# Cross attention of a fused decoder: power per projection, context rounding and output projection later, input quantisation over two groups

## What is computed

```python
def _div_clamp_fp8(x, scale):
    y = jnp.clip(x / scale, -448.0, 448.0)
    y = y.astype(jnp.bfloat16).astype(jnp.float32)
    return y.astype(jnp.float8_e4m3fn).astype(jnp.float32)
def _fp8_linear_pertensor(x, wq, w_scale, in_scale):
    xq = _div_clamp_fp8(x, in_scale)
    return jnp.einsum('bsi,oi->bso', xq * in_scale, wq) * w_scale
...
ln_out = _ln(hidden_states, ln_w, ln_b)
q = _ln(_fp8_linear_pertensor(ln_out, wq, ...).reshape(b, s, g, hpg, d), qln_w, qln_b)
k = _ln(_fp8_linear_pertensor(ln_out, wk, ...).reshape(b, s, g, d), kln_w, kln_b)
v = _fp8_linear_pertensor(ln_out, wv, ...).reshape(b, s, g, d)
core = _gqa(q, k, v).reshape(b, s, nh * d)
qx = _ln(_fp8_linear_pertensor(ln_out, wqx, ...).reshape(b, s, g, hpg, d), qxln_w, qxln_b)
kx, vx = jnp.split(jnp.einsum('bsi,oi->bso', cond, w_kv_x), 2, axis=-1)
kx = _ln(kx.reshape(b, sc, g, d), kxln_w, kxln_b)
xout = _gqa(qx, kx, vx.reshape(b, sc, g, d)).reshape(b, s, nh * d)
catq = _div_clamp_fp8(jnp.concatenate([core, xout], axis=-1), proj_smooth)
return jnp.einsum('bsi,oi->bso', catq, wproj) * (proj_in_scale * proj_w_scale)
```

## Time and profile before

| | us |
|---|---|
| median of 3 runs | 1294.21 |
| lowest, highest | 1289.71, 1295.01 |
| the profiled execution | 1295.41 |
| its span in the profile | 1293.6 |
| PE / DVE / ACT / POOL busy | 1026.7 / 902.1 / 607.4 / 448.1 |
| mean granted TensorE clock | 0.907 of full |

### The profile page before, as it was taken

The page is one execution under the profiler, slowest core; times in us unless marked ns, Lnnn a source line. Parts: engine busy times, 40 slices in busy tenths (PEclk is TensorE's granted clock), DMA queues, the critical chain, the costliest instruction groups (busy, mean ns, idle before and its releaser), DMA issues.

```text
span 1293.6 us, 15285 instructions
## 1 busy us (share of the span) xinstructions
PE 1026.7 (79%) x5194; PEld 639.5 (49%) x5204; DVE 902.1 (70%) x1501; ACT 607.4 (47%) x1457; POOL 448.1 (35%) x247
## 2 busy tenths in 40 slices
PE   5998876365556766477878899899887799999998
PEld 3777732124122222245556566666655465555555
DVE  4567689887699998887887877676888444333222
ACT  2444461065566651365566667777566223111111
POOL 0012244050076640256666645445554422000000
PEclk9879789777778787699999999999998899999999
DMA  9500000401000000000000062000003000000000
GB/s 339 220 1 1 1 0 0 133 15 26 0 1 1 0 0 1 1 1 1 1 1 2 1 159 66 2 1 2 1 1 115 1 1 1 1 17 1 1 1 17
DMA packets 23773, 36.56 MB, mean 28 GB/s; under 512 B 3584, under 2 KB 19904, under 8 KB 22592
## 3 DMA queue, kind: packets, MB, share of 16 engines
q1 hardware_dynamic: 23696, 35.58, 8.4%
HBM read 34.53 MB, written 1.05 MB: 28 GB/s over the span
## 4 chain that ended last, share of the span: by engine, by line
PE 37%; DVE 22%; ACT 10%; issue 8%; POOL 1%; DVEq 0%; ACTq 0%; POOLq 0%
PE ps L2150 12%; PE ps L2174 8%; DVE arena L979 6%; PE ps L1725 3%; DVE arena L975 3%; PE ps L1709 3%; ACT arena L1024 3%; PE ps L1699 2%; PE ps L1692 2%; ACT arena L2004 2%; DVE arena L1831 2%; PE ps L1738 2%; DVE arena L1825 2%; PE ps L2162 1%; PE ps L1717 1%
## 5 line engine op out<-in xcount | busy, mean ns | idle before, releaser
L2198 DVE TENSOR_TENSOR arena<-arena,ps 128x512 f32<-128x512 f32 (+1 forms) x56 | 38.5, 687 | 151.3 <-ACT arena L2238 151.3
L2238 ACT ACTIVATE arena<-ps,arena 128x512 f32<-128x512 f32 (+1 forms) x56 | 38.4, 687 | 167.5 <-PE ps L2150 167.5
L1058 PE MATMUL ps<-arena,ident 128*128 128x512 f32 x128 | 83.9, 791 | 37.6 <-DVE arena L984 37.6
L1995 ACT ACTIVATE arena<-ps,arena 128x512 f32<-128x512 f32 x96 | 68.1, 775 | 88.3 <-PE ps L1699 88.0
L2174 PE MATMUL ps<-wide,arena 128*128 128x256 f32 (+1 forms) x448 | 106.2, 380 | 0.0
L2066 POOL TENSOR_TENSOR arena<-arena 128x1024 f32<-128x1024 bf16 x32 | 67.9, 2122 | 107.8 <-DVE arena L1638 107.8
L2077 POOL TENSOR_TENSOR arena<-arena 128x12 f32<-128x12 f32 x32 | 73.1, 2283 | 91.9 <-DVE arena L1836 91.7
L2004 ACT ACTIVATE arena<-ps,arena 128x128 f32<-128x128 f32 x256 | 91.1, 383 | 22.8 <-DVE arena L1816 22.8
L2150 PE MATMUL ps<-XT,wide 128*128 128x512 f16 (+1 forms) x384 | 93.3, 380 | 0.6 <-DVE X L1866 0.6
L2174 PEld LDWEIGHTS ps<-wide,arena 128*128 128x128 f32 (+1 forms) x448 | 84.9, 190 | 17.7 <-issue 1.6
L1717 PE MATMUL ps<-ident,arena 128*128 128x128 f32 x256 | 44.0, 297 | 56.1 <-DVE arena L1825 55.7
(11 more groups left out here) (319 smaller groups left out, 2439.2 us busy)
## 6 DMA issues: line engine op xcount, KB each, us to landing
side<-in_wproj SPq DMA_DIRECT2D x1, 4096.0 KB, 14.2
wide<-in_w_down SPq DMA_DIRECT2D x1, 3584.0 KB, 12.7
wide<-in_w_gate SPq DMA_DIRECT2D x2, 1728.0 KB, 12.1
side<-in_w_up SPq DMA_DIRECT2D x3, 1024.0 KB, 9.3
arena<-in_taps SPq DMA_DIRECT2D x1, 2048.0 KB, 15.7
wide<-in_wq SPq DMA_DIRECT2D x1, 2048.0 KB, 10.6
wide<-in_wqx SPq DMA_DIRECT2D x1, 2048.0 KB, 16.0
wide<-in_w_kv_x SPq DMA_DIRECT2D x1, 2048.0 KB, 24.0
```

The source lines that it names most:

```text
L1058: last = pe.matmul(ps[:, 4 + 2 * c + j, :], k.ident[:, :], read[i % 2][:, 512 * j:512 * j + 512], start=(n == 0), stop=(n == NST - 1), ski ...
```

## The change

Power: `root` is called per projection, with 4 columns each; the keys' epsilon is added on POOL, those of the queries stand as a 129th column in the squares' tile, so that the reduction adds them, and `sum_eps` goes. DVE does `variance(g+1, 1)` between the two `biggest`, and `variance(g+1, 2)` behind both `divide`. ACT does `square(g+1, 2)` behind `weigh(g, 1)`. POOL does the three `root` first and then `add_c(g-1)`, `round_c(g-1)`; `cm` has two buffers. `project_out(g, 0)` moves from turn g+1 to turn g+2. `scale_x` moves to even groups, behind `clip`, `quantise_x` and `add_x` stay in odd groups (`quantise_x` behind `clip`, `add_x` a group earlier than before), `round_x` stays in even groups, now behind `round_c`. `turn_x` and `take_x` move a turn. `add_out` and the experts' variance move behind `normalise`.

```diff
FP8_ROUND = 1.5 * 2.0 ** 20
 FP8_LEAST = 2.0 ** -6
 NEG = -1e30
-MOE_AT = 15296
+MOE_AT = 15824
 def wait(eng, sem, n):
...
     xq = [A.take([3, KC * S], BF16) for _ in range(2)]
     xqx = k.XT[:, 1, :].bitcast(BF16).rearrange("p (b n) -> p b n", b=B)
     qn = A.take([3, BLK])
-    sq = A.take([2, BLK])
+    sq = A.take([2 * MAXB, HD + 1])
     sq_k = A.take([MAXB, HD], BF16)
...
     cy = A.take([QH, S], BF16)
-    cm = A.take([QH, S], BF16)
+    cm = [A.take([QH, S], BF16) for _ in range(2)]
     cs = A.take([QH, S])
     cq = [A.take([QH, S], BF16) for _ in range(2)]
     norms = A.take([8])
...
     xq_ready = k.sem("xa_xq_ready")
     proj_psum = k.sem("xa_proj_psum")
     sq_ready = k.sem("xa_sq_ready")
-    var_ready = k.sem("xa_var_ready")
     rs_ready = k.sem("xa_rs_ready")
     qn_ready = k.sem("xa_qn_ready")
     turn_psum = k.sem("xa_turn_psum")
...
         for j in range(3):
             turn(0, j)
         turn_x(1)
+        turn_x(2)
         for g in range(NG):
             nxt = g + 1 < NG
             if nxt:
...
                 moe.turn_comb(pe, 0, ps[:, 6, :])
             turn_p(g, 0)
             if g >= 2:
-                project_out(g - 2, 1)
+                project_out(g - 2, 0)
             turn_p(g, 1)
             mix(g, 0)
+            if g >= 2:
+                project_out(g - 2, 1)
             mix(g, 1)
-            if g >= 1:
-                project_out(g - 1, 0)
             if nxt:
                 for j in range(3):
                     turn(g + 1, j)
-            if g % 2 == 0 and g // 2 + 2 < B:
-                turn_x(g // 2 + 2)
+            if g % 2 and (g + 5) // 2 < B:
+                turn_x((g + 5) // 2)
             if g == 25:
                 moe.total_tensor(pe, ps[:, 6, :])
             if g in (26, 27):
                 moe.logits(pe, 0, g - 26, ps[:, 6, :])
+        project_out(NG - 2, 0)
         project_out(NG - 2, 1)
         project_out(NG - 1, 0)
         project_out(NG - 1, 1)
...
             dve.tensor_tensor(p[t], p[t], rden[:, t, :].unsqueeze(2).broadcast_to([P, MAXB, S]),
                               ALU.mult).then_inc(pn_ready, 1)
+        def eps_columns(path, j):
+            link(dve.tensor_copy(sq[:, (j - 1) * MAXB:j * MAXB, HD], eps_sq[:, path, j, :]))
+
         def variance(g, j):
             dve.wait_ge(sq_ready, 3 * g + j + 1)
-            wait(dve, rs_ready, g)
-            dve.tensor_reduce(var[:, j, :], sq[:, j - 1, :].rearrange("p (h d) -> p h d", d=HD), AX.X,
-                              ALU.add).then_inc(var_done, 1)
-
-        def sum_eps(g):
-            dve.wait_ge(var_done, 2 * g + 2)
-            dve.tensor_tensor(var, var, eps_sq[:, place(g)[0], :, :], ALU.add).then_inc(var_ready, 1)
+            if g == 2 * B:
+                eps_columns(1, j)
+            wait(dve, rs_ready, 3 * (g - 1) + j + 1)
+            dve.tensor_reduce(var[:, j, :], sq[:, (j - 1) * MAXB:j * MAXB, :], AX.X, ALU.add).then_inc(var_done, 1)
         def normalise(g, j):
-            dve.wait_ge(rs_ready, g + 1)
+            dve.wait_ge(rs_ready, 3 * g + j + 1)
             wait(dve, turn_psum, 3 * (g - 1) + j + 1)
             dve.tensor_tensor(qn[:, j, :].rearrange("p (h d) -> p h d", d=HD),
                               ps[:, j, :].rearrange("p (h d) -> p h d", d=HD),
...
         def clip(g):
             dve.wait_ge(cy_raw, 2 * g + 2)
             link(dve.tensor_scalar(flat(cy), flat(cy), FP8_MAX, -FP8_MAX, ALU.min, ALU.max))
-            wait(dve, cq_ready, g)
-            fp8_vector(dve, link, flat(cy), flat(cm)).then_inc(cy_ready, 1)
+            wait(dve, cq_ready, g - 1)
+            fp8_vector(dve, link, flat(cy), flat(cm[g % 2])).then_inc(cy_ready, 1)
         def add_out(n):
             b = n % B
...
         link(dve.reciprocal(out_scale, w.ranged[:, 6:7]))
         link(dve.tensor_scalar(out_scale, out_scale, w.proj_scale[:, 0:1], w.proj_scale[:, 1:2], ALU.mult, ALU.mult))
         dve.sem_inc(consts, 1)
+        eps_columns(0, 1)
+        eps_columns(0, 2)
         k.norm_vector(dve, link, 7, batches=rest)
         variance(0, 1)
         variance(0, 2)
-        sum_eps(0)
         dve.wait_ge(k.xn_ready, 5 * B + 1)
         k.norm_stats(dve, link, k.XN, rest)
         for j in range(3):
...
         for g in range(NG):
             nxt = g + 1 < NG
             biggest(g, 0)
+            if nxt:
+                variance(g + 1, 1)
             biggest(g, 1)
             divide(g, 0)
+            divide(g, 1)
             if nxt:
-                variance(g + 1, 1)
                 variance(g + 1, 2)
-                sum_eps(g + 1)
-            divide(g, 1)
-            if g % 2 == 1 and g > 2:
-                add_out((g - 3) // 2)
-                if g > 2 * B + 3 and g != 27:
-                    stats_of((g - 3) // 2 - B - 1)
-            if g % 2 == 1 and (g + 3) // 2 < B:
-                scale_x((g + 3) // 2)
-                quantise_x((g + 3) // 2)
-            if g == 25:
-                stats_of(3)
-                moe.var_vector(dve, 0)
             if g == 27:
                 moe.ranges_vector(dve, link)
             if g >= 27:
...
             if nxt:
                 for j in range(3):
                     normalise(g + 1, j)
+            if g % 2 == 1 and g > 2:
+                add_out((g - 3) // 2)
+                if g > 2 * B + 3 and g != 27:
+                    stats_of((g - 3) // 2 - B - 1)
+                if g == 25:
+                    stats_of(3)
+                    moe.var_vector(dve, 0)
             smoothed(g, 0)
             smoothed(g, 1)
             clip(g)
+            if g % 2 == 0 and (g + 4) // 2 < B:
+                scale_x((g + 4) // 2)
+            if g % 2 == 1 and (g + 3) // 2 < B:
+                quantise_x((g + 3) // 2)
             if g == 25:
                 moe.total_vector(dve, link, ps[:, 6, :])
                 moe.normalise(dve, 0, 0)
...
         def take_x(b):
             act.wait_ge(lnT_psum, b + 1)
-            wait(act, xy_ready, b)
+            wait(act, xy_raw, b)
             for c in range(KC):
                 last = act.activation(lnT[:, c, :], ps[:, 6, c * P:(c + 1) * P], ACT.Identity,
                                       scale=ln_w[:, c:c + 1], bias=ln_b[:, c:c + 1])
...
         def square(g, j):
             act.wait_ge(proj_psum, 4 * g + j + 1)
-            wait(act, rs_ready, g)
             if j == 0:
+                wait(act, rs_ready, 3 * (g - 1) + 1)
                 for i in range(MAXB):
...
             else:
-                act.activation(sq[:, j - 1, :], ps[:, j, :], ACT.Square).then_inc(sq_ready, 1)
+                wait(act, var_done, 2 * (g - 1) + j)
+                act.activation(sq[:, (j - 1) * MAXB:j * MAXB, 0:HD], ps[:, j, :].rearrange("p (h d) -> p h d", d=HD),
+                               ACT.Square).then_inc(sq_ready, 1)
         def take_v(g):
             act.wait_ge(proj_psum, 4 * g + 4)
...
         for j in range(3):
             take_turned(0, j)
         take_x(1)
+        take_x(2)
         for g in range(NG):
             nxt = g + 1 < NG
             if nxt:
...
             weigh(g, 0)
             if nxt:
                 square(g + 1, 1)
+            weigh(g, 1)
+            if nxt:
                 square(g + 1, 2)
-            weigh(g, 1)
             take_pT(g, 0)
             if nxt:
                 take_v(g + 1)
...
             if nxt:
                 for j in range(3):
                     take_turned(g + 1, j)
-            if g % 2 == 0 and g // 2 + 2 < B:
-                take_x(g // 2 + 2)
+            if g % 2 and (g + 5) // 2 < B:
+                take_x((g + 5) // 2)
             if 18 <= g < 25:
                 moe.square(act, 2 * (g - 18))
                 moe.square(act, 2 * (g - 18) + 1)
...
     def gpsimd(pool, link):
         def add_x(b):
             pool.wait_ge(xy_ready, b + 1)
+            wait(pool, xq_ready, b)
             pool.tensor_tensor(flat(xs), flat(xy), flat(xm), ALU.add).then_inc(xs_ready, 1)
         def round_x(b):
...
         def add_c(g):
             pool.wait_ge(cy_ready, g + 1)
-            pool.tensor_tensor(flat(cs), flat(cy), flat(cm), ALU.add).then_inc(cs_ready, 1)
+            wait(pool, cq_ready, g)
+            pool.tensor_tensor(flat(cs), flat(cy), flat(cm[g % 2]), ALU.add).then_inc(cs_ready, 1)
         def round_c(g):
             pool.wait_ge(cs_ready, g + 1)
             wait(pool, w_used, g - 1)
-            pool.tensor_tensor(flat(cq[g % 2]), flat(cs), flat(cm), ALU.subtract).then_inc(cq_ready, 1)
-
-        def root(g):
-
-            pool.wait_ge(var_ready, g + 1)
-            wait(pool, qn_ready, 3 * g)
-            pool.tensor_tensor(rs, var, minus_half, ALU.pow).then_inc(rs_ready, 1)
+            pool.tensor_tensor(flat(cq[g % 2]), flat(cs), flat(cm[g % 2]), ALU.subtract).then_inc(cq_ready, 1)
+
+        def root(g, j):
+
+            if j == 0:
+                pool.wait_ge(sq_ready, 3 * g + 1)
```

(18 more changed lines are left out.)

## The result

| | before | after |
|---|---|---|
| median, us | 1293.51 (4 runs) | 1333.37 (4 runs) |
| lowest, highest | 1289.71, 1295.01 | 1327.28, 1337.24 |
| the profiled execution, span | 1295.41, 1293.6 | 1334.60, 1332.8 |
| mean granted TensorE clock | 0.907 | 0.886 |

The ratio of after to before is 1.0308, 95% interval 1.0262 to 1.0355: slower by 3.1%, 39.9 us. The forecast was 1334.

The account below looks back on a forecast made before the run. No engine is saturated; a turn is a ring through four engines. Groups 0 to 14 +23, 15 to 18 +3, 19 to 25 +8, tail +2, clock +4: +40 on 1294.2 gives 1334 us, range 1312 to 1352.

Parts of the forecast that it names:

- DVE's order: biggest(g, 1) behind variance(g+1, 1) waits for ACT's square; weigh(g, 1) starts at 4.19 for 3.11 today.
- b: Zero point of the times in a turn of the group loop: the start of biggest(g, 0) on DVE.
- on PE alone: PE's chain per turn: turn_p(g, 1) at 6.78 against 6.16, each turn 0.6 us longer, 11.39 to the next project.
- rival D: Faster, 1274: DVE's ring regains its 24 us, some 20 counting, if the last power ends by b+6.6; chance 0.05.
- Power: POOL's split root: about 0.9 us more work a turn, hidden; last power 7.40 to 8.41, ending 0.8 later than today's.
- Rounding: On POOL add_c and round_c follow the last power, 8.41 to 12.74; DVE waits, smoothed at 10.62, clip meets round_c.
- ring of 13.97: Root, add_c, round_c, clip, biggest through POOL and DVE: closes at 13.97 us whatever PE does.
- four times 0.79: Groups 15 to 18, path 1: the DVE-POOL ring of 13.97 rules over PE's 13.79; +3 us.
- Input quantisation: Path 0: quantise_x makes odd groups 15.35; round_x ending at 15.9 delays project, making even groups 17.85.
- Clock: TensorE's clock falls while PE waits 4.5 us before project in even groups: 0.7 for six of them, +4 us.
- Rival B: PE falls to the lower clock elsewhere too, about 2 us in groups 19 to 25: +16, 1350; chance 0.12.
- Tail: Groups 26 to 31: about +1 each, +2 for experts' subtractions, less some 6 for freed routing: +2, between -5 and +6.

Follow-up runs that it names:

- both other orders of POOL: The changed kernel with round_x at the head of POOL's even turn, 1318.24 us; the changed kernel with add_c and round_c first again, powers behind, 1349.59 us.
- the last experiment: Kernel before plus power per projection, add_x a group earlier, and context rounding behind the powers from group 24 on only: 1272.52 us, ratio 0.9821.

## Why the prediction was right, step by step

**DVE's order: right in mechanism, small in price.** The walk through the turn was within 0.2 us at each step up to the power. After b, forecast and measured in group 8: variance 2.82, 2.75; `biggest(g, 1)` 3.46, 3.35; `weigh(g, 1)` 4.19, 4.07; multiply 6.01, 5.83; last power 7.40, 7.20; `smoothed` 10.62, 10.40; end of `round_c` 12.74, 12.50. But the text sized this order as 0.6 a turn "on PE alone" and laid the rest of the loss to the rounding. The runs share it out otherwise: the order costs 20.5 alone, almost all of it from group 19 on, and 44.7 together with the rounding, of which 21.9 in groups 0 to 14. The point of decision that rival D named was the end of the last power; what moves it is this order.

**Power: sign wrong when read alone.** The text counted "the last is 0.8 later" as a cost. Alone it is worth 9.8 us, in the changed order 37. The step failed in taking the whole delay of the last power as the power's: it belongs to `biggest` and `variance`.

**Rounding.** The ring of 13.97 was 13.63 on path 1, so +2.1 for the forecast's 3. (Its "four times 0.79" should be 0.76, 13.97 less 13.21; the 3 stays.) In odd groups it was 14.89 for 15.35.

**Input quantisation.** With the clock kept up even groups are 17.12, forecast 17.85; in the kernel after itself none is below 17.4. `round_x` ended at 15.08 after b in group 8 and not at 15.9: DVE's instructions in between stretched POOL's by 0.18 and 0.17 (0.85 for 0.67, 1.81 for 1.64), not by 0.3 each, and the earlier steps were 0.24 ahead.

**Clock.** Forecast 4 for six even groups; 6.7 by the kernel with PE kept busy. With it the even groups sum to 109.6 (forecast 107.1 + 4), the odd ones to 89.4 (92.1), group 0 to 14.27 (13.55), the last two to 28.5 (28.0): 241.7 for 240.8 + 4. In groups 19 to 25 two turns, with a granted clock of 1.00, take 14.82 and 14.98 (15.15 forecast), but four, with 0.89, take 16.1 to 16.3. Rival B's mechanism is there, in four turns of seven, for some 5 us of the 10.3. (B's own sum was 18, so 1352 and not the 1350 written.) Two turns of this stretch, PE, the second with the clock down:

```profile
866.32 0.66 PE L1716 MATMUL ps<-ident,arena 128*128 128x128 f32 x4 [2.38 <-DVE arena L1826]
866.82 1.04 PE L1737 MATMUL ps<-side,arena 128*128 128x256 f16 x8
...
881.21 0.76 PE L1716 MATMUL ps<-ident,arena 128*128 128x128 f32 x4 [2.38 <-DVE arena L1826]
881.76 1.91 PE L1737 MATMUL ps<-side,arena 128*128 128x256 f16 x8
```

and the windows over these two places, in the columns of the first fence:

```profile
881.20:884.20 3.00, 2.99 (x16) 2.49 (x17) 2.25 (x5) 2.24 (x7) 0.69 (x1) 0.57 0.00 0
866.30:869.30 3.00, 2.85 (x20) 2.34 (x21) 2.24 (x5) 2.83 (x8) 0.68 (x1) 1.00 0.03 5
```

The granted clock is 0.57 in one, so nearly all of it at 1.2 GHz, and 1.00, 2.4 GHz, in the other; the wait ahead of both was the same.

**Tail.** +3.6 for the forecast's 2. The gain from routing that the rounding no longer holds is real (6.3 us from group 24 on in the last experiment), and was eaten by the ring. That was weighed, as "some 6", with the right sign.

**Rival D, faster.** 21.6 of its 24 us did come back on DVE, and the kernel was slower all the same. "No order of POOL repairs" it: right, both other orders of POOL stayed slower than before (1318, 1350). The order of DVE does.

**The total.** +40 was forecast and +39.9 measured, but the terms were off by -3.5 on path 0 (clock counted in), -0.9, +2.3 and +1.6. So the agreement is partly errors that cancel.

## What to carry to other kernels

On an engine that works strictly in order, look at what a step waits for before it is put in front of another: here DVE idled 2 us for ACT's square with the scores ready, and the delay ran through three engines. Long POOL work is free only as long as nobody waits for its end; behind the last link of the ring it becomes part of it, so check where the ring closes before work is moved to "later". Try parts of a large change one by one, in the old kernel as well as in the new one: here two parts gained 18 us, and what was bundled with them cost 58.
